# Mask conversions and bias rows at other places in the first two stages, and the last layer's scores from h and h(Wq Wk^T)

## The reference

```python
Q = h @ Wq;  K = h @ Wk;  V = h @ Wv        # each W is 256 x 256
S = Q @ K.T
mask = nan_to_num(-inf * (1.0 - (A + eye)))
x = x + softmax(S + mask, axis=1) @ V
```

## Time and profile before

| what | value |
|---|---|
| three runs | 2544.5, 2546.5, 2548.12 us; median 2546.5 |
| the profiled execution | 2546.07 us, its span 2544.1 us |
| mean granted TensorE clock | 0.959 |
| `opening` | 0 to 77.4 us |
| `first_layer` | 77.4 to 989 us |
| layer 1 | 989 to 1322.7 us |
| layer 2 | 1322.7 to 1839 us, its loop 1399.8 to 1806 |
| layer 3 | 1839 to 2544.1 us |
| busy: TensorE, VectorE, ScalarE, GpSimd | 2285.7, 1830.3, 1400.8, 112.3 us |
| conversions `mask_d<-in_adj` | 8, median 23.6 us from issue to landing |

### The profile page before, as it was taken

How to read it: one execution, slowest core, us unless ns; L and a number is a source line. 1 busy time by engine, 2 the same in 40 slices (tenths; PEclk the granted TensorE clock), 3 DMA queues, 4 the chain that set the end, 5 groups by cost and what they waited for, 6 DMA issues and landing times. The chain is left out here.

```text
span 2544.1 us, 46073 instructions
## 1 busy us (share of the span) xinstructions
PE 2285.7 (90%) x17238; PEld 1716.5 (67%) x17238; DVE 1830.3 (72%) x2947; ACT 1400.8 (55%) x2240; POOL 112.3 (4%) x125
## 2 busy tenths in 40 slices
PE   4579999999999984999967999899799999999998
PEld 3457777778677753888855777777546666666667
DVE  4487687786887943111128898888589988988896
ACT  4365555656646534666646454454346555655565
POOL 1000010000100100000000000000000000000000
PEclk8799999999999987999988999999899999999999
DMA  7741422414101102222211111112111111111100
GB/s 164 119 59 36 65 49 63 80 40 78 47 30 43 43 25 87 84 86 78 82 46 36 65 62 61 66 62 70 45 59 36 49 44 41 43 50 45 32 30 26
DMA packets 63223, 147.78 MB, mean 58 GB/s; under 512 B 10055, under 2 KB 14810, under 8 KB 62045
## 3 DMA queue, kind: packets, MB, share of 16 engines
q1 hardware_dynamic: 56749, 111.62, 14.0%
q0 software_dynamic: 5760, 33.56, 7.9%
q10 hardware_dynamic: 560, 0.52, 0.1%
HBM read 170.82 MB, written 41.96 MB: 84 GB/s over the span
## 5 line engine op out<-in xcount | busy, mean ns | idle before, releaser
L1878 PE MATMUL bank<-VB,ph 128*128 128x257 f16 x2048 | 522.3, 280 | 97.8 <-DVE VB L1822 33.2
L1879 PE MATMUL bank<-VB,ph 128*128 128x257 f16 x2048 | 521.2, 279 | 0.0
L195 PE MATMUL bank<-s_row,kT_hi 128*128 128x512 f16 x1024 | 307.9, 383 | 6.6 <-DMA s_row<-qT_d 4.7
L1390 PE MATMUL bank<-VA,ph 128*128 128x257 f16 x1024 | 282.3, 276 | 24.7 <-DVE VA L1060 24.7
L1878 PEld LDWEIGHTS bank<-VB,ph 128*128 128x128 f16 x2048 | 203.9, 100 | 143.2 <-DVE pl L1817 54.4
L1882 PE MATMUL bank<-VB,pl 128*128 128x257 f16 x1024 | 290.1, 283 | 0.0
L2484 PE MATMUL bank<-VA,ph 128*128 128x257 f16 x1024 | 280.6, 274 | 3.0 <-ACT w_later_hi L2345 2.4
L1391 PE MATMUL bank<-VA,ph 128*128 128x257 f16 x1024 | 282.0, 275 | 0.0
L1392 PE MATMUL bank<-VA,pl 128*128 128x257 f16 x1024 | 282.0, 275 | 0.0
L2486 PE MATMUL bank<-VA,pl 128*128 128x257 f16 x1024 | 280.3, 274 | 0.0
L2485 PE MATMUL bank<-VA,ph 128*128 128x257 f16 x1024 | 280.1, 274 | 0.0
(11 more groups left out here) (327 smaller groups left out, 4703.6 us busy)
## 6 DMA issues: line engine op xcount, KB each, us to landing
mask<-mask_d SPq DMA_DIRECT2D x256, 256.0 KB, 2.7
mask_d<-in_adj POOLq DMA_DIRECT2D x8, 2048.0 KB, 23.6
xg<-x SPq DMA_DIRECT2D x16, 512.0 KB, 4.3
x<-xo POOLq DMA_DIRECT2D x16, 512.0 KB, 2.9
xg<-in_x SPq DMA_DIRECT2D x8, 512.0 KB, 11.7
w_d<-wr SPq DMA_DIRECT2D x8, 512.0 KB, 2.6
f<-w_d SPq DMA_DIRECT2D x8, 512.0 KB, 8.8
x<-xg SPq DMA_DIRECT2D x8, 512.0 KB, 3.9
```

The source lines that it names most:

```text
L195: last = nc.tensor.matmul(out_ap, st, mv, start=(i == 0), stop=(i == len(todo) - 1))
L1390: nc.tensor.matmul(acc, ph[:, u % HR, c], v_row(V, 0, t), start=(t == 0), stop=False)
L1878: nc.tensor.matmul(acc, p_hi, v_at(V, 0, t), start=first, stop=False)
L1879: last = nc.tensor.matmul(acc, p_hi, v_at(V, 1, t), start=False, stop=final and not weighted)
```

## The change

In the opening, the first conversion goes behind the fifth root and a wait for all dense weights; `cut_bias` moves from after group 1 to after group 5; the weight pieces move one group later on ScalarE and VectorE. In `first_layer`, GpSimd waits for the first three mask loads and the gate weights, then issues at the head of iteration i the conversion of group i + 1 instead of i + 2. In layer 1's first group, Wq and Wk are loaded into a tile of their own and transposed; their product Wqk = Wq Wk^T is made and cut. In layer 2 `hT` is written to `kT` directly, there is one product, `qT` = Wqk^T h^T, and `v` is made from slices of `kT` that move with the loop. Layer 3 is unchanged.

```diff
-    later = [("W1", K, D), ("W2", K, D + 1), ("Wq", K, D), ("Wk", K, D), ("Wv", K, D)]
+    later = [("W1", K, D), ("W2", K, D + 1), ("Wv", K, D), ("Wqk", K, D)]
# opening, GpSimd
-                    root(2)
-                    nc.gpsimd.dma_start(mask_d[0:P, :], a["adj"][0:P, :]).then_inc(s_mst[0], 16)
-                    for g in range(3, G):
+                    for g in range(2, G):
                         root(g)
+                        if g == 4:
+                            pool.wait_ge(s_w, 16 * len(dense_in))
+                            nc.gpsimd.dma_start(mask_d[0:P, :], a["adj"][0:P, :]).then_inc(s_mst[0], 16)
# opening, ScalarE
-                        if 2 <= g < 2 + pieces:
-                            if g == 2:
+                        if 3 <= g < 3 + pieces:
+                            if g == 3:
                                 act.wait_ge(s_w, 16 * len(dense_in))
# opening, VectorE
                         take_columns(g)
-                        if 3 <= g < 3 + pieces:
...
-                        if g == 1:
+                        if 4 <= g < 4 + pieces:
+                            cut_weights(g - 4)
+                        if g == 5:
                             cut_bias()
# first_layer, GpSimd
-                    nc.gpsimd.dma_start(mask_d[P:2 * P, :], a["adj"][P:2 * P, :]).then_inc(s_mst[1], 16)
                     for x_ in opened:
                         pool.sem_clear(x_)
+                    for n in range(MS):
+                        pool.wait_ge(s_mq[n], 16)
+                    pool.wait_ge(s_gate, 16 * 3)
                     for i in range(G + 2):
-                        if i + 2 < G:
-                            nc.gpsimd.dma_start(mask_d[(i + 2) * P:(i + 3) * P, :], ...
+                        if i + 1 < G:
+                            nc.gpsimd.dma_start(mask_d[(i + 1) * P:(i + 2) * P, :], ...
# layer 1, first group
             def act_make(q):
+                if q == 2:
+                    nc.scalar.wait_ge(qk_turned.sem, qk_turned.upto(0))
+                    nc.scalar.copy(qkT[0][:, :, :], psum[:, 4:6, :]).then_inc(qkT_hi.sem, 1)
                 if q == 4:
                     nc.scalar.wait_ge(folded.sem, folded.upto(2 * K - 1))
-                    nc.scalar.copy(w_later[0][:, :], later32[:, :]).then_inc(later_hi.sem, 1)
+                    nc.scalar.copy(w_later[0][:, 0:own], later32[:, 0:own]).then_inc(later_hi.sem, 1)
+                    nc.scalar.wait_ge(qk_made.sem, qk_made.upto(0))
+                    nc.scalar.copy(w_later[0][:, own:own + K * D], bank[6][:, :]).then_inc(later_hi.sem, 1)
+            def pe_make(q):
+                if q == 1:
+                    nc.tensor.wait_ge(s_later, 16 * 6)
...
+                                last = nc.tensor.transpose(bank[4 + m][:, at:at + P], qk32[:, i, k, m * P:(m + 1) * P],
+                                                           ident[:, :])
+                if q == 3:
+                    nc.tensor.wait_ge(qkT_lo.sem, qkT_lo.upto(0))
+                    for k in range(K):
...
+                        last = products(nc.tensor, bank[6][:, k * D:(k + 1) * D], ...
# layer 2, ScalarE and VectorE
-                        hi(hT[0][:, k, :], bank[4 + k][:, :], "hT", k)
+                        hi(kT[0][:, k, ds(g * GW, GW)], bank[4 + k][:, :], "hT", k)
...
-                    for k in range(K):
-                        act.wait_ge(pe_s.sem, pe_s.at(g, "kT", k))
-                        hi(kT[0][:, k, ds(g * GW, GW)], bank[6 + k][:, :], "kT", k)
...
-                        lo(kT[1][:, k, c], bank[6 + k][:, :], kT[0][:, k, c], "kT", k)
# layer 2, TensorE
-                    for name, b in (("q", 4), ("k", 6)):
...
+                    c = ds(g * GW, GW)
+                    for m in range(K):
+                        products(pe, bank[4 + m][:, :],
+                                 [(w("Wqk", k, m * P, (m + 1) * P), (kT[0][:, k, c], kT[1][:, k, c]))
+                                  for k in range(K)]).then_inc(pe_s.sem, pe_s.one("qT", m))
                 if q == 6:
-                    pe.wait_ge(dve_s.sem, dve_s.at(g, "kT", K - 1))
+                    pe.wait_ge(dve_s.sem, dve_s.at(g, "qT", K - 1))
                     for r in range(R):
-                        products(pe, bank[4 + r][:, 0:D], [(cols(hT, k, r), w("Wv", k)) for k in range(K)]
+                        c = ds(g * GW + r * P, P)
+                        products(pe, bank[4 + r][:, 0:D], [((kT[0][:, k, c], kT[1][:, k, c]), w("Wv", k)) ...
```

More of the change, by code:

```diff
@@ L538, in _ @@
                         take_columns(g)
-                        if 3 <= g < 3 + pieces:
-                            dve.wait_ge(weights_hi.sem, weights_hi.upto(g - 3))
-                            nc.vector.tensor_tensor(piece(w_dense[1], g - 3), piece(dense32, g - 3),
-                                                    piece(w_dense[0], g - 3), ALU.subtract).then_inc(weights_lo.sem, 1)
-                        if g == 1:
+                        if 4 <= g < 4 + pieces:
+                            cut_weights(g - 4)
+                        if g == 5:
                             cut_bias()
+                    for i in range(G - 4, pieces):
+                        cut_weights(i)
                 @block.tensor
@@ L1884, in quad @@
                             last.then_inc(pe_q.sem, pe_q.one("pv", r))
-                    groups(pe, quad, work["pe"])
+                    groups(pe, quad, work["pe"], work.get("pe_make"))
             loaded[0] += G * Q // MS
@@ L1931, in finish_layer1 @@
             junk = sb(mem, "junk2", [P, 2 * K, D], F32)
+            qk32 = sb(mem, "qk32", [P, 2, K, D], F32)
+            qkT = [sb(mem, f"qkT_{p}", [P, K, 2 * D], F16) for p in ("hi", "lo")]
+            own = where["Wqk"][1]
             src_col = sb(mem, "src_col", [P, K], F32)
@@ L1935, in finish_layer1 @@
             src_hi = Count(sem("src_hi"))
+            qk_turned, qkT_hi, qkT_lo, qk_made = (Count(sem(n)) for n in ("qk_turned", "qkT_hi", "qkT_lo", "qk_made"))
             def later(name):
@@ L1949, in act_make @@
             def act_make(q):
+                if q == 2:
+                    nc.scalar.wait_ge(qk_turned.sem, qk_turned.upto(0))
+                    nc.scalar.copy(qkT[0][:, :, :], psum[:, 4:6, :]).then_inc(qkT_hi.sem, 1)
                 if q == 4:
                     nc.scalar.wait_ge(folded.sem, folded.upto(2 * K - 1))
-                    nc.scalar.copy(w_later[0][:, :], later32[:, :]).then_inc(later_hi.sem, 1)
+                    nc.scalar.copy(w_later[0][:, 0:own], later32[:, 0:own]).then_inc(later_hi.sem, 1)
[5 more added lines that the diff above has]
+                    for m in range(K):
+                        for i in range(2):
+                            for k in range(K):
+                                at = i * D + k * P
+                                last = nc.tensor.transpose(bank[4 + m][:, at:at + P], qk32[:, i, k, m * P:(m + 1) * P],
+                                                           ident[:, :])
+                    last.then_inc(qk_turned.sem, 1)
+                if q == 3:
+                    nc.tensor.wait_ge(qkT_lo.sem, qkT_lo.upto(0))
+                    for k in range(K):
+                        rows = slice(k * P, (k + 1) * P)
+                        last = products(nc.tensor, bank[6][:, k * D:(k + 1) * D],
+                                        [((qkT[0][:, m, rows], qkT[1][:, m, rows]),
+                                          (qkT[0][:, m, D:2 * D], qkT[1][:, m, D:2 * D])) for m in range(K)])
+                    last.then_inc(qk_made.sem, 1)
             def dve_make(q):
@@ L2042, in pe_part @@
                     pe.wait_ge(dve_s.sem, dve_s.before(g, "d", R - 1))
+                    pe.wait_ge(later_lo.sem, later_lo.upto(1))
                     for k in range(K):
@@ L2077, in finish_layer2 @@
             h = w_gate[1][:, 0:2 * R * D].bitcast(F32)
-            hT = [sb(mem, f"h2T_{p}", [P, K, GW], F16) for p in ("hi", "lo")]
             qT = sb(mem, "qTg", [P, 2, K, GW], F16)
@@ L2161, in dve_part @@
                         lo(qT[:, 1, k, :], bank[4 + k][:, :], qT[:, 0, k, :], "qT", k)
-                    for k in range(K):
-                        dve.wait_ge(act_s.sem, act_s.at(g, "kT", k))
-                        c = ds(g * GW, GW)
-                        lo(kT[1][:, k, c], bank[6 + k][:, :], kT[0][:, k, c], "kT", k)
                 if q == 7:
```

42 lines of the change are left out of this document (27 added, 15 removed).

## The result

The changed kernel takes **2481.05 us** (median of four runs, 2478.31 to 2482.04), the kernel before 2547.31 beside it (2544.5 to 2552.55): a ratio of 0.9736, 95% interval 0.9718 to 0.9754. The forecast was 2486.0 in a range of 2472 to 2504. The profiled executions are 2478.31 and 2546.07 us, so the pair of traces differs by 67.8 us where the sum had 60.5.

What follows compares the result with a forecast made beforehand. TensorE was taken to bound the kernel (90% busy), with waits in the opening and layer 0's first iteration and VectorE near-bound in layer 2. -18 - 27 + 2.5 - 18 = -60.5 from 2546.07 gives 2486 us, range 2472 to 2504.

Steps and rivals of the forecast that it cites:

- The opening: Block before layer 0: later conversion and bias rows start make_h(4) 18.6 us sooner, 0.5 lost to column loads; -18 us.
- The head: Start of layer 0's stream: VectorE's 27.0 us of waits under two conversions go, so ex comes sooner; -27 us.
- The margin of the fifth mask: Layer 0's head: fifth mask, loaded under the one conversion, lands at 34 us into the block, due at 35.
- Layer 1: TensorE's first group: 8 added transposes and 12 products all count, 2.3 to 4.6 us; +2.5 us taken.
- Layer 2: Removed products, casts and subtractions save 8 x 2.8 us, less 4.2 for moving addresses; -18 us.
- The row-to-row price of 2.8 a group: Layer 2: VectorE's next p comes 2.81 us late behind the kT subtractions; TensorE loses 2.6 at the same point.
- The 4.2 us for the moving addresses: Layer 2: register operations for TensorE's moving kT reads cost 0 to 1.1 us a group; 0.6 x 7 taken.
- Late transfers (1): Opening and head: late column loads cost 3 us, bias rows 3, masks under the conversion 7; 2499 us, chance 0.17.
- (2), the addresses: Layer 2 gives 5 us instead of 18, from dearer moving addresses or longer waits for v; 2499 us, chance 0.08.
- (3), all covers hold: Opening -21, head -31, layer 2 -23, layer 1 +2; 2473 us, chance 0.11.
- (4), the clock: Layer 2: shorter bursts keep TensorE at 1.2 GHz for whole groups, +37 us each; up to 2763 us, chance 0.03.
- even shares: Layer 0's head: by even turns of the queues a mask needs about twice its 2.7 us, leaving 15 to spare.

Runs made afterwards that it cites:

- e4: Kernel before with only the first conversion moved behind the fifth root and the dense weights; bias rows and weight pieces at their old places: 2526.97 us.
- e8: Changed kernel with the opening's weight pieces at their old places and the bias rows cut after group 2: 2479.35 us.
- e12: Changed kernel with the wait for three masks and the gate weights kept, but two conversions behind it (groups 1 and 2): 2490.13 us.
- e1: Kernel before with the change of the opening and of layer 0's head only; layers 1 and 2 as before: 2499.44 us.
- e2: Changed kernel with the opening and layer 0 as before, so only the changed scores of layers 1 and 2: 2525.45 us.
- e7: Changed kernel, but layer 2 reads kT at the fixed columns of group 0 for every group, without moving addresses: 2482.31 us.
- e9: Changed kernel with the 12 removed products per group of layer 2 put back on TensorE only: 2502.72 us.
- e10: Changed kernel with two subtractions of 512 columns per group of layer 2 put back on VectorE only: 2501.91 us.
- e6: Changed kernel without GpSimd's waits for the first three masks and the gate weights before the one conversion: 2487.63 us.
- e5: Kernel before with the change of layer 0's head alone; opening as before: 2518.05 us.

## Why the prediction came out right, step by step

- **The opening, -18 forecast, -18.0 in the pair of traces.** Each link held: weights at 27.4 (28), `make_h(4)` at 30.65 (30.2), end at 59.4 (59). The column loads did not stick, so the 0.5 us I had put on them was not needed. What I did not see is that one of the two edits did it all (e4).
- **The head, -27 forecast, -25.5 measured.** The argument, that `ex` comes sooner by what VectorE no longer waits and that the rest is the same work, held: from `ex` to iteration 1 it is 66.68 us (66.67 before). Two terms that I set to zero come to 2.0 us, of which 0.5 came back in small pieces: the first `p` stands 0.5 us further behind the barrier, and a wait of 1.52 us for `whT_hi` appears where ScalarE had been ahead during the old stalls. GpSimd's wait let the conversion go 11.4 us into the block, not 8 (the last gate weights land at 70.4); it landed at 35 all the same, as it took 23.4 us and not 25. The margin of the fifth mask, 1 us by the forecast, measured 1.4; it was gone in e8 and with a second conversion (e12).
- **Layer 1, +2.5 forecast, 2.2 by e1 against e2.** The 0.9 in the pair of traces is luck of the clock, which rose 2.9 us after the first product in one and 5.4 in the other: over the nine kernels with the edit layer 1 takes 327.2 us on the mean, over the five without 324.7, +2.4. ScalarE itself waits twice for TensorE's new work (2.41 us before its first new cast, 1.82 before the second), off the path: TensorE's only wait over 0.3 us in these two groups is one of 0.9 for `ag` in each, as in the kernel before.
- **Layer 2, -18 forecast, -20.0 in the loop and -0.8 behind it.** The row-to-row price of 2.8 a group was right: 2.85 by the table, over all kernels with and without the edit. Two terms were mis-sized. The 4.2 us for the moving addresses measured 0.1 (e7). The last group gave 0.8 by the table's means (2.1 in the pair) instead of 2.8: `v` does end 2.8 us earlier against the last `rden` than in the kernel before, 1.4 than in e1, but layer 3 then waits for a transfer. Here TensorE's first scores of layer 3, in the changed kernel:

```profile
1777.65 1.03 PE L195 MATMUL bank<-s_row,kT_hi 128*128 128x512 f16 x2 [6.26 <-DMA s_row<-qT_d]
```

  In e1 that wait is 4.81 us. The forecast had the pair of engines right: work had to leave both (e9, e10).
- **Layer 3, 0 forecast.** -1.9 in the pair of traces, but the same instructions take 692.5 to 692.6 us in four kernels, 694.2 in seven and 695.8 to 696.2 in three. The three values go with TensorE's clock. Here 3 us of the table of busy time 45 us behind layer 3's first `VB`, in the kernel before and in the changed one (the granted clock is the third number from the end):

```profile
1893.00:1896.00 3.00, 3.00 (x9) 1.03 (x7) 0.32 (x1) 0.00 (x0) 0.00 (x0) 0.50 0.00 0
```

```profile
1827.40:1830.40 3.00, 2.63 (x11) 0.97 (x8) 1.19 (x1) 0.33 (x1) 0.00 (x0) 1.00 0.00 0
```

  The kernels at 695.8 to 696.2 have such a stretch at 1.2 GHz there, worth 1.5 to 1.9 us up to the first `rden`, and another in the last group, worth 1.7; those at 694.2 have only the second, those at 692.5 neither. It isn't without order by edit: all six kernels with the scores as changed and nothing put back have 694.2, the five with the old scores 692.5 (three) or 695.8 and 696.2. What sets it was not tested. By the table's means the change is worth 18.3 + 25.3 - 2.4 + 20.0 + 0.8 = 62.0 us; the forecast had 60.5. The medians of the runs say 66.3, or 64 against the 2545 us that the kernel before took beside the later runs. The pair's 67.8 is above the 62.0 mainly because layer 1 (1.5 us), the gap (1.3) and layer 3 (1.9) fell well in it; that is luck, and no merit of the sum.
- **The rivals.** Late transfers (1) did not come, but e12 and e8 show how near they were. (2), the addresses, fell. (3), all covers hold, came true for the addresses of layer 2; its -23 there was not reached (-20.8). (4), the clock, did not hold whole groups at 1.2 GHz; a light form of it was there before the change and is there in e10.
- **The two pages.** From the turns of the queues that the Trainium skill describes ("DMA: Bandwidth & Descriptors", "Queues, rings and completion order"), the prediction made even shares, and an estimate of 5.4 us for the fifth mask; it took 20.6, and under two conversions the sixth took 32.1. The row that I kept to was the better number. But the trace agrees with the page's rule as it is worded, a packet from each in turn; the step from turns to even shares was wrong, as the last section shows with the packets. From the queue of 64 that "TensorE: Matmul & The Clock Gate" of the Trainium skill gives in its table of specifications, the prediction took that the register operations would vanish; e7 agrees with the result, though it doesn't show the depth of the queue. By that page the estimate would have been 2482.

## What to carry to other kernels

A large transfer in the background is best priced by what is issued beside it: find out which small loads are issued within its 25 us, and let it go when the last of them that anyone waits for has landed. Count packets, not bytes: a load behind it needs as many turns as it has packets on a DMA engine. Where two engines are both near the bound, take the row-to-row distance on the later one as the price, and put the work back on each alone to see that both paths carry it. Read a change's price from landmarks of its own stage over several kernels, since stages that nothing touched moved by 3 us and more, and look up the granted clock of the stretches compared.

## What the runs showed of the hardware that was not expected

**A load under a conversion gets one packet for each of the conversion's.** In e6 the conversion is issued at 61.93 us and lands 26.9 us later, at 88.8. The masks issued from 59.3 to 60.2 land in 3.1 to 3.8 us, `th` (61.11) in 8.1, but `ag` (61.59) in 27.0 and `gy` (62.10) in 28.6, at 88.6 and 90.7. In the changed kernel the conversion lands at 94.4; the fifth mask, issued 3 us behind it at 74, takes 20.6 us and lands at 94.6, the sixth, issued at 83.3, takes 11.8 and lands at 95.2. They end together, whatever their time of issue. The packets show why. Below are the DMA queues of e12 from 98 to 113.3 us, GpSimd's and then SyncE's (packets, MB, share of 16 engines), while the second conversion runs and masks wait behind it:

```profile
q0 software_dynamic: 96, 1.57, 95.4%
q1 hardware_dynamic: 96, 0.20, 3.8%
```

Each queue moved 96 packets, 6 on each of the 16 DMA engines in 15.3 us, so a turn takes 2.55 us. But a packet of the conversion is 16 KB and takes 2.4 us, one of a mask 2 KB and 0.1 us. A mask of 256 KB is 128 packets, 8 on each DMA engine: 8 turns, 20.4 us by this, an estimate, against 20.6 measured. A gate weight has 16 a DMA engine, more than the conversion's 8, and so lands when the conversion ends; what SyncE issued later lands behind it. e12 fits as well: its fifth mask, issued at 74.0 behind both conversions, lands at 97.6, a turn after the first of them (94.9) and long before the second (115.3); the sixth lands 17.9 us after the fifth.

**SyncE's stall moves.** The same queue of issues, behind the same early conversion, sticks at `lng` for 17.52 us in the kernel before and among the bias rows in e5, where two issues take 20.95 us and the opening is 2.2 us longer:

```profile
24.03 20.95 SPq L323 DMA_DIRECT2D brow<-in_L_gnn_g_b  x2
```

**Layer 2's period goes with the clock.** TensorE waits for `pl` once a group. Below is that wait in a steady group of the changed kernel and, from the table of busy time, the 4 us around and behind it (the granted clock is the third number from the end); then the same two for a steady group of e10.

```profile
1546.23 0.28 PE L1886 MATMUL bank<-VB,ph 128*128 128x257 f16 x1 [2.27 <-DVE pl L1825]
```

```profile
1546.00:1550.00 4.00, 3.77 (x35) 3.35 (x36) 4.00 (x8) 3.48 (x7) 0.00 (x0) 1.00 0.22 66
```

```profile
1546.84 0.40 PE L1886 MATMUL bank<-VB,ph 128*128 128x257 f16 x1 [3.83 <-DVE pl L1825]
```

```profile
1546.80:1550.80 4.00, 3.96 (x19) 2.80 (x20) 4.00 (x7) 3.44 (x8) 0.00 (x0) 0.50 0.22 66
```

After the wait of 2.27 us the clock stays at 2.4 GHz, after that of 3.83 it is 1.2 for the next 4 us. Now whole groups, from one group's `p` to the next: the first two of the changed kernel that are shown above, then three in a row of e10.

```profile
1413.67:1471.04 57.37, 51.46 (x430) 42.75 (x429) 50.31 (x89) 27.70 (x49) 2.16 (x3) 0.94 0.20 64
1471.04:1525.75 54.71, 50.40 (x431) 42.42 (x429) 50.28 (x89) 27.70 (x49) 2.15 (x3) 0.97 0.21 67
```

```profile
1413.82:1469.26 55.44, 48.97 (x430) 41.34 (x429) 51.47 (x92) 27.73 (x49) 2.16 (x3) 1.00 0.21 66
1469.26:1526.37 57.11, 50.66 (x431) 42.19 (x429) 51.51 (x91) 27.71 (x49) 2.15 (x3) 0.97 0.20 64
1526.37:1584.25 57.88, 51.45 (x431) 42.61 (x429) 51.50 (x92) 27.73 (x49) 2.15 (x3) 0.94 0.20 63
```

So the changed kernel's group of 57.4 us is the one at a clock of 0.94, and its steady groups of 54.7 have 0.97. In e10 the groups slow down from 55.4 to 57.9 us as the clock falls from 1.00 to 0.94, with the same work. The kernel before alternates between 57.3 us at 0.97 and 58.9 at 0.94. e10 adds 1.2 us of work a group, and its steady groups are 3.2 longer than the changed kernel's; between its own groups at 1.00 and at 0.94 the difference is 2.4. VectorE there also waits up to 2.5 us for `kT_hi`. At the same 0.97, e10's group is still 2.4 longer than the changed kernel's and not 1.2; where in the group the clock is low may matter, and no run takes that apart. The length of the wait for `pl` alone does not settle the clock: in e10's group of 55.4 a wait of the same 3.83 us, at 1434.29, was followed by full clock.
